# Thirteen of 53 clearing transfers moved from SyncE's queue to ScalarE's in a four-layer graph network

## The reference

```
h = relu(layernorm(x)); x = x + L0(h)      # and likewise L1, L2, L3
L0: g  = gelu([h[row], h[col]] @ mlp_w1 + mlp_b1)          # per edge, 64 wide
    ew = sigmoid(g @ mlp_w2 + mlp_b2)                      # weight of the edge
    deg = segment_sum(ew, col); dinv = rsqrt(deg)
    out = segment_sum((h @ conv_w)[row] * dinv[row] * ew * dinv[col], col) + conv_b
L1: two GCN convolutions;  L2: message passing with two MLPs;  L3: three GCN convolutions
```

## Time and profile before

| what | value |
|---|---|
| time, median of 3 runs | 5044.58 us (5042.11 to 5046.07) |
| span of the profiled execution (the page gives no other time for it) | 5064.6 us |
| busy share: TensorE, VectorE, GpSimd, ScalarE | 74%, 47%, 43%, 16% |
| moved by DMA | 928.52 MB, 183 GB/s on the mean |

### The profile page before, as it was taken

One profiled execution on the slowest core, in us unless ns is written; L12 is line 12 of the kernel. 1 busy time (PEld: TensorE's weight loads), 2 busy tenths in 40 slices (PEclk: granted clock), 3 DMA queues, 4 the chain that ended last, 5 costly groups with the idle time before them and its releaser, 6 DMA issues.

```text
span 5064.6 us, 81513 instructions
## 1 busy us (share of the span) xinstructions
PE 3723.9 (74%) x26476; PEld 2540.4 (50%) x26476; DVE 2360.9 (47%) x11373; ACT 810.4 (16%) x2506; POOL 2186.7 (43%) x1749
## 2 busy tenths in 40 slices
PE   3444443333333566669999698899999999999999
PEld 2333332222222455556666365566666666666666
DVE  6555554444344899983323226734443333332111
ACT  1122111111111455550000002211110000000000
POOL 3556566777777888888888850000000000000000
PEclk7555555555555799989999899999999999999999
DMA  4888886555455799947777673455555665665665
GB/s 126 306 295 290 295 289 188 127 133 136 119 130 130 181 231 234 233 97 174 178 200 170 142 189 96 122 158 167 168 163 181 190 191 179 190 191 179 199 198 168
DMA packets 557026, 928.52 MB, mean 183 GB/s; under 512 B 175004, under 2 KB 412012, under 8 KB 549836
## 3 DMA queue, kind: packets, MB, share of 16 engines
q1 hardware_dynamic: 389580, 833.79, 51.8%
q0 software_dynamic: 162496, 87.75, 12.0%
q10 hardware_dynamic: 4544, 1.77, 0.2%
HBM read 741.60 MB, written 181.47 MB: 182 GB/s over the span
## 4 chain that ended last, share of the span: by engine, by line
PE 42%; another core or an unknown queue 19%; POOL 16%; issue 10%; DVE 6%; DMA 4%; ACT 2%; SPq 0%; ACTq 0%; DVEq 0%; POOLq 0%
PE ps L1012 35%; POOL adj L662 15%; DMA adj<-count,place 4%; PE ps L1046 1%; PE ps L1022 1%; POOL rows L654 1%; PE ps L998 1%; DVE same L1276 1%; PE ps L922 1%; ACT tanh_half L730 1%; ACT gelu L725 1%; PE ps L1058 1%; PE ps L913 1%; PE ps L1035 1%
## 5 line engine op out<-in xcount | busy, mean ns | idle before, releaser
L1012 PE MATMUL ps<-parts,halves 128*128 128x384 bf16 x14602 | 2487.8, 326 | 50.4 <-DMA halves<-adj 44.6
L1012 PEld LDWEIGHTS ps<-parts,halves 128*128 128x128 f16 x14602 | 1431.4, 98 | 936.3 <-issue 49.8
L662 POOL DMA_INDIRECT adj<-count,place x832 | 1317.8, 1584 | 265.3 <-issue 237.2
L654 POOL DMA_INDIRECT rows<-table,src_of x880 | 843.9, 959 | 514.6 <-issue 243.3
L922 PE MATMUL ps<-dst_mlp,onehot_t 128*128 x2640 | 367.6, 232 | 693.4 <-ACT onehot_t L720 400.6
L1476 DVE TENSOR_REDUCE summed_f<-ps 128x128 f32<-128x384 f32 x335 | 186.7, 557 | 1444.1 <-PE ps L1022 1129.5
L922 PEld LDWEIGHTS ps<-dst_mlp,onehot_t 128*128 128x128 bf16 x2640 | 274.8, 104 | 776.2 <-issue 715.6
L807 ACT COPY source_t<-ps 128x128 f32<-128x128 f32 x196 | 52.2, 266 | 1825.0 <-PE ps L1035 1819.5
L720 ACT COPY onehot_t<-ps 128x512 bf16<-128x512 bf16 x220 | 128.9, 586 | 1331.0 <-remote 1157.4
L936 PE MATMUL ps<-weight_parts,onehot_b 128*128 128x4 bf16 x880 | 130.9, 184 | 260.1 <-DVE weight_parts L1339 130.3
L753 ACT ACTIVATE onehot<-plain,norm 128x128 f32<-128x128 bf16 x880 | 280.9, 390 | 227.8 <-DVE norm L1382 125.8
(11 more groups left out here) (250 smaller groups left out, 3476.7 us busy)
## 6 DMA issues: line engine op xcount, KB each, us to landing
halves<-adj SPq DMA_DIRECT2D x289, 800.0 KB
halves<-adj SPq DMA_DIRECT2D x253, 768.0 KB
adj<-slot_of SPq DMA_DIRECT2D x53, 1568.0 KB
h_rows<-rows SPq DMA_DIRECT2D x220, 256.0 KB
rows<-h_rows SPq DMA_DIRECT2D x220, 256.0 KB
spare_sum<-key_list SPq DMA_DIRECT2D x104, 512.0 KB
onehot_list<-onehot_b SPq DMA_DIRECT2D x220, 128.0 KB
low_row<-low_list SPq DMA_DIRECT2D x220, 128.0 KB
```

The lines of the kernel that those rows point to most:

```text
L654: nc.gpsimd.indirect_dma_start(out=rows_0[:, g % RING, s, :], out_offset=None, in_=table[:, :], in_offset=bass.IndirectOffsetOnAxis(ap=src ...
L662: nc.gpsimd.indirect_dma_start(out=adj[:, :], out_offset=bass.IndirectOffsetOnAxis(ap=place[:, k:k + 1], axis=0), in_=count16[:, k:k + 1], ...
L1012: last = nc.tensor.matmul(ps_sum[u % 3], halves[:, n % AR, c - at, :], parts[q % 2][:, c, :, :].rearrange("p t d -> p (t d)"), start=(c == ...
```

## The change

The SyncE loop now clears blocks 13 to 52 and is done with it at group 78; ScalarE begins the clears of blocks 0 to 12 in the 13 turns of `take_first_part`, ahead of that stage's wait. The count that GpSimd waits for, and the group at which it begins to scatter, stay as they were.

```diff
                 for n in runs_begun(g + 3) if g + 3 < GROUPS else ():
                     load_keys(sp, n)
-                if g % 2 == 0 and g // 2 < BLOCKS:
-                    sp.dma_start(adj_rows[g // 2, :, 0:DB * P], zero16).then_inc(zeroed, 16)
+                if g % 2 == 0 and g // 2 < BLOCKS - MC:
+                    sp.dma_start(adj_rows[MC + g // 2, :, 0:DB * P], zero16).then_inc(zeroed, 16)
...
             def take_first_part(i):
                 b0, b1 = node_blocks(i)
+                act.dma_start(adj_rows[i, :, 0:DB * P], zero16).then_inc(zeroed, 16)
                 act.wait_ge(src_mlp_set, i + 1)
                 nc.scalar.copy(dst_mlp[:, b0:b1, 0, :], ps_node[:, i % 2, 0:b1 - b0, MH:2 * MH]).then_inc(first_parts, 1)
 
+            act.wait_ge(zero_set, 1)
             pipeline(MC, [(2, take_first_part), (0, relu_nodes), (0, copy_nodes)])
```

## The result

| | median, us | runs |
|---|---|---|
| before, beside it | 5045.32 (5042.11 to 5050.92) | 10 |
| changed kernel | 5058.88 (5053.31 to 5061.80) | 10 |
| ratio | 1.0026, 95% interval 1.0017 to 1.0035 | |

The changed kernel is 13.6 us slower (0.26%; the interval reaches from 0.17 to 0.35%). Its profiled execution took 5057.46 us, with a span of 5055.7.

What follows compares the result with a forecast made beforehand. GpSimd's gathers, then its scatters, were taken to gate TensorE's adjacency passes. SyncE's loss 0, ScalarE's issues 0 and the delayed table stores +7.6 us, on 5044.6, gave 5052 us; range 5041 to 5070.

Steps and rivals of the forecast that it cites:

- The pace does not depend on the clears: First pass: GpSimd's waits end 12.45 us apart among the clears, 12.90 behind them, so removing clears there gains nothing.
- The cushion of 9.83 us: GpSimd's wait after its first 24 gathers, until 132.60 us, ahead of its seventh group; it absorbs that much delay.
- The first term: Node table: 13 clears fill the DMA engines, delay the table stores and make the first gather 25 us late.
- The bound of 4.2 us from the loads: Lower end of the first gather's delay: loads on two queues landed in 6.9 us, a lone store in 2.7.
- the rival in which the stores keep their turn: Table stores are delayed only 4.2 us, under the cushion, so nothing reaches the pass: 5044.6 us; chance 0.30.
- 40.1: Upper delay in us of the first gather if table stores finish last at 296 GB/s; that rival: 5064.6 us, chance 0.24.
- The 2.7 us under the lower bound: Landing time of a table store taken to be on an idle machine, set against 6.9 us beside loads.
- if a row is a packet: DMA queues: a 512-byte store row would wait behind a 12.5 KB clear row each time, supporting the main case or stores-last.
- the 15.3 us: How late GpSimd's seventh group would start, with the first gathers 25.1 us late and the wait ahead of it gone.
- the middle, 7.6 us: Part of the seventh group's delay expected at the last gather, halfway between nothing and all; main case, chance 0.36.
- Within 0.2%: Outcome of no change that the runs can tell, less than 10.1 us either way; chance 0.57.
- the 116 forecast: Sign in the changed kernel's profile: GpSimd's first gather starts near 116 us instead of 90.67.

Runs made afterwards that it cites:

- extra_clears: Kernel before with all 53 clears left on SyncE, plus 13 more of the same shape by ScalarE to an unread buffer: 5080.38 us, ratio 1.0035.
- gathers_8us_late: Kernel before with 12 idle GpSimd writes between the last table store and the first gather, no clear moved: 5059.00 us, ratio 0.9990.
- eight_clears: Changed kernel, but ScalarE takes only eight of the clears and SyncE the other 45: 5046.26 us, ratio 1.0000 against the unchanged kernel.
- clears_after_table: Changed kernel, but ScalarE begins its 13 clears only when the node table is stored: 5087.56 us, ratio 1.0043 against the unchanged kernel.
- gathers_20us_late: Kernel before with 32 idle GpSimd writes between the last table store and the first gather, no clear moved: 5080.43 us, ratio 1.0034.
- after_again: The changed kernel, unaltered, profiled a second time on a chip of the upper level: 5077.19 us, ratio 1.0028 against the unchanged kernel.
- clears_in_small_rows: Changed kernel with each of ScalarE's 13 clears written as 14 rows of 896 bytes instead of one of 12544: 5061.47 us, ratio 1.0034.
- key_store_in_two: ScalarE's 13 clears begun after the table is stored, and the key list's store split, its first 64 KB alone: 5067.94 us, one run.
- before_again: The kernel before, unaltered, profiled a second time on a chip of the upper level: 5061.30 us, ratio 0.9996.

## Why the prediction was right in its direction and low in its size

**Right.** The loss comes over the path that the prediction named: table store, first gather, seventh group, last gather. The pace does not depend on the clears (the 12.2 us above; extra_clears loses no more than the change). Their removal from groups 80 to 104 is worth nothing that can be measured, the issue on ScalarE is hidden, and the scatters start as they did. The cushion of 9.83 us is real: gathers_8us_late and eight_clears lose nothing.

**The first term.** "I take 25 us" for the first gather's delay; it measured 19.4, and 20.9 on the upper level. The bound of 4.2 us from the loads, and with it the rival in which the stores keep their turn, is refuted for 13 clears; 40.1 is too. The 2.7 us under the lower bound were misread: that store was issued at 76.98 among the table's, not on an idle machine. The sum behind the 25 us left something out: SyncE was held in issuing. The split store fits turns of some kind, but not of one row each: its first eight rows took 1.35 us each and the other 48 took 0.42, and one row of a clear takes 0.50 us (an estimate: 12.5 KB at a sixteenth of the 403 GB/s that clears_after_table moved from 120 to 150 us). How such turns are weighed stays open. By the Trainium skill ("DMA: Bandwidth & Descriptors", section "Queues, rings and completion order") an engine goes round its queues packet by packet, a packet being typically some 9 to 17 descriptors, each an order to move one piece; the prediction's "if a row is a packet" isn't what that section says, and no run here shows how many rows go in one turn.

**The step that failed in size** is this one: "What of the 15.3 us reaches the last gather lies between nothing … and everything …: No row shows the loop beside a GpSimd that gathers without a pause, so I take the middle, 7.6 us." On the chips of the upper level nothing or little was worn off. In gathers_20us_late 25.5 less the cushion of 10.45 is 15.0, and 17.2 stand at the last gather; in after_again 10.5 are due and 12.4 stand there; in clears_after_table 23.3 of 27.6 do. With everything instead of half, the forecast's own delay gave 15.3, and the measured one 9.6 to 10.5 and some 2 us on top; the medians say 13.6 and 16.2. The too large first term and the too small second one partly cancelled in the 7.6 us; that it lies no further off is in part luck.

On the lower level some was worn off. No trace of the unchanged kernel was taken there, but eight_clears, which loses nothing, can stand for it, with its eighth group and its last gather at:

```profile
140.34 0.94 POOL L654 DMA_INDIRECT rows<-table,src_of  x1 [0.30 <-issue]
...
1639.78 1.15 POOL L654 DMA_INDIRECT rows<-table,src_of  x1 [0.30 <-issue]
```

The changed kernel's last gather:

```profile
1645.19 1.10 POOL L654 DMA_INDIRECT rows<-table,src_of  x1 [0.30 <-issue]
```

Against eight_clears the changed kernel is 10.2 us late at the eighth group and 5.4 at the last gather (it isn't on record whether the two chips are the same); on eight_clears's own chip clears_in_small_rows is 16.9 and then 13.6 late, key_store_in_two 26.2 and then 19.5. So half to four fifths was kept there and nearly all on the upper level. Why the chips differ in this stays open, and so does the way of the result's own 13.6 us through the pass, since its pair has no two traces on one chip.

Why the loop doesn't catch up at its start is seen and not explained: a GpSimd that starts late gathers seven groups on end (110.09 to 145.48), and from 132.3 us on, while that run lasts, VectorE's loop mostly stands. Two windows of the changed kernel, columns as in the earlier trace rows:

```profile
130.00:140.00 10.00, 2.09 (x16) 1.60 (x16) 2.02 (x13) 2.29 (x3) 7.56 (x9) 0.50 1.05 409
140.00:150.00 10.00, 0.00 (x0) 0.00 (x0) 1.29 (x5) 0.12 (x1) 4.26 (x5) 0.50 0.56 209
```

The same of before, where GpSimd paused until 132.60:

```profile
130.00:140.00 10.00, 4.95 (x36) 3.54 (x36) 8.15 (x52) 3.37 (x6) 5.69 (x6) 0.50 1.07 413
140.00:150.00 10.00, 4.34 (x32) 3.26 (x32) 6.47 (x39) 2.17 (x6) 5.69 (x6) 0.50 1.04 393
```

Between 130 and 150 us VectorE works 3.31 us instead of 14.62. The transfers are as full in both (1.05 and 1.07 from 130 to 140), so they don't explain it, and neither do ScalarE's clears, since gathers_20us_late has none and the same wait. The gathers alone don't either: from 127.45 to 132.3 VectorE compares keys beside them. In the changed kernel's timeline above, VectorE's multiplication of line 1318 ends at 141.30; the reduction of line 1322, which in the first group needs nothing but that product, starts at 146.91, 1.4 us after GpSimd's last gather of that run ended (145.48). I read it so, without a test: GpSimd's run takes the place of the pause in which before did its first groups. What in the chip makes VectorE stand was not tried.

**The chances.** "Within 0.2%" had 0.57 and 0.26% was measured, with an interval that reaches to either side of the bound; "slower" had 0.38. Taking the middle between nothing and everything is what put it there.

**The other signs named.** That GpSimd's waits would be shorter until it has caught up was wrong on the upper level (151.6 for 136.7 us). The wait ahead of the seventh group is gone, as said. The first gather at 110.09 lies 6 us ahead of the 116 forecast and well above the 101 from which the prediction would have fallen. Groups 80 to 104 took 6.25 us each in the changed kernel, under the 6.3 that was named as a sign of being wrong; but its groups 20 to 80, with clears, took 6.26, and on the upper level groups 80 to 104 took 6.34 in after_again for 6.29 in before_again, so it is the level and not the removal.

## What to carry to other kernels

A low DMA share in one stretch is no free room if a short store in that stretch gates the next stage: before moving bulk transfers there, find that store and measure the cushion between it and the first wait that hangs on it; up to the cushion (here about 10 us, eight clears of thirteen) the move costs nothing. Two equal windows with and without the transfers told beforehand that nothing could be gained at the old place, whatever the DMA row of the page looked like. Don't assume that a pipeline in a steady state works off a delay at its start, even where one engine waits in every second turn: here half to all of it was carried through 220 groups, by the chip.

## What the runs showed of the hardware that was not expected

- An issue is not only some 0.4 us: beside another queue's clears SyncE stood 11.02, 13.94 and 9.05 us in one store's issue each, and ScalarE up to 6.79 us when each clear was made of small rows.
- A store of 448 KB went from 4.1 to 29.9 us beside 13 clears of 1568 KB that ScalarE had begun 30 us earlier.
- The same kernel took 5044 to 5047 us on one chip and 5061 to 5064 on two others, more than the change costs. The traces part mostly late in the first pass: eight_clears on the first chip and before_again on another start group 100 within 0.1 us of each other and their last gathers 12.9 us apart.
